# Cross-attention layer on one core: all 32 row tiles by seven half-size score products per pair, and the V side as whole float32 products

## The reference, cut to what matters

```python
Q = (img_embed @ Wq)...; K = (sent_embed @ Wk)...; V = (sent_embed @ Wv)...   # per head
score = einsum('bhqd,bhkd->bhqk', Q, K) / sqrt(D)
attn  = softmax(where(mask, score, -inf))
ctx   = einsum('bhqk,bhkd->bqhd', attn, V).reshape(B, -1, H * D)
out   = ctx @ Wo + img_embed
return (out - mean) * rsqrt(var + EPS) * gamma + beta
```

## Time and profile before

| | |
|---|---|
| median of three runs | 364.62 us |
| profiled execution, own time | 364.46 us |
| its span, first to last instruction | 362.6 us |
| TensorE busy | 353.9 us (98%) |
| VectorE / ScalarE / GpSimd busy | 296.4 (82%) / 238.3 (66%) / 193.1 (53%) |
| mean granted TensorE clock | 0.996 |

### The profile page before, as it was taken

One profiled execution on the slowest core, in us unless ns is written; L12 is line 12 of the kernel. 1 busy time (PEld: TensorE's weight loads), 2 busy tenths in 40 slices (PEclk: granted clock), 3 DMA queues, 4 the chain that ended last, 5 costly groups with the idle time before them and its releaser, 6 DMA issues.

```text
span 362.6 us, 6839 instructions
## 1 busy us (share of the span) xinstructions
PE 353.9 (98%) x2326; PEld 329.0 (91%) x2326; DVE 296.4 (82%) x516; ACT 238.3 (66%) x767; POOL 193.1 (53%) x180
## 2 busy tenths in 40 slices
PE   8999999999999999999999999899999999999993
PEld 5999999999999998999899988889988998998873
DVE  3489999998878587887888787797977978889886
ACT  3377757776876565765677667677768768767550
POOL 0046644654455212445355667597696696784234
PEclk9999999999999999999999999999999999999998
DMA  8998679966733310314234052231431423412012
GB/s 259 413 422 312 227 265 372 337 229 259 249 116 122 114 57 3 131 46 156 78 116 144 32 174 85 92 101 75 174 106 70 163 64 123 146 61 87 29 60 87
DMA packets 19682, 55.81 MB, mean 154 GB/s; under 512 B 1728, under 2 KB 3264, under 8 KB 17728
## 3 DMA queue, kind: packets, MB, share of 16 engines
q1 hardware_dynamic: 18784, 54.38, 42.2%
q10 hardware_dynamic: 864, 1.00, 0.9%
HBM read 46.98 MB, written 8.39 MB: 153 GB/s over the span
## 4 chain that ended last, share of the span: by engine, by line
PE 88%; DMA 4%; ACT 3%; DVE 2%; POOL 1%; issue 1%; POOLq 0%; DVEq 0%; ACTq 0%
PE pair L381 28%; PE pair L556 27%; PE pair L484 14%; PE pair L496 13%; PE pair L543 5%; DMA w_out<-wq_t 3%; PE pair L469 1%; DMA w_proj<-wk 1%; ACT prob L693 1%; ACT prob L715 1%; POOL out_sb L1158 1%; ACT centred L762 1%; PE pair L388 1%; PE pair L514 0%; DVE centred L1041 0%
## 5 line engine op out<-in xcount | busy, mean ns | idle before, releaser
L1205 POOL TENSOR_TENSOR w_proj_lo<-w_proj,w_proj_hi 128x768 fp32r<-128x768 f32 x26 | 47.9, 1866 | 61.1 <-ACT w_proj_hi L645 61.1
L693 ACT ACTIVATE prob<-masked,neg_max 128x77 f32<-128x77 f32 x128 | 44.2, 347 | 38.6 <-DVE neg_max L916 38.6
L381 PE MATMUL pair<-kv_t,w_out_hi 128*128 128x308 f32 x240 | 63.0, 335 | 0.3 <-DVE w_out_lo L849 0.3
L1158 POOL TENSOR_TENSOR out_sb<-centred,beta_sb 128x512 f32<-128x512 f32 x31 | 40.0, 1292 | 42.4 <-ACT centred L762 42.4
L556 PE MATMUL pair<-vw_hi,pt_hi 128*128 128x512 f32 x155 | 61.7, 398 | 0.0
L556 PE MATMUL pair<-vw_hi,pt_lo 128*128 128x512 f32 x155 | 60.8, 392 | 0.0
L556 PE MATMUL pair<-vw_lo,pt_hi 128*128 128x512 f32 x155 | 60.8, 392 | 0.0
L849 DVE TENSOR_TENSOR w_out_lo<-w_out,w_out_hi 128x1024 fp32r<-128x1024 f32 x30 | 49.3, 1682 | 4.9 <-ACT w_out_hi L653 4.4
L381 PE MATMUL pair<-kv_t,w_out_lo 128*128 128x154 f32 x240 | 48.8, 244 | 0.0
L381 PEld LDWEIGHTS pair<-kv_t,w_out_hi 128*128 128x128 f32 x240 | 42.2, 189 | 0.7 <-issue 0.7
L381 PEld LDWEIGHTS pair<-kv_t,w_out_lo 128*128 128x128 f32 x240 | 42.5, 189 | 0.0
(11 more groups left out here) (116 smaller groups left out, 954.8 us busy)
## 6 DMA issues: line engine op xcount, KB each, us to landing
w_out<-wo SPq DMA_DIRECT2D x8, 1024.0 KB, 5.1
xt_in<-x_tiles SPq DMA_DIRECT2D x16, 512.0 KB, 4.0
x_in<-x_rows SPq DMA_DIRECT2D x16, 512.0 KB, 4.6
out<-out_sb SPq DMA_DIRECT2D x31, 256.0 KB, 2.1
w_out<-wq_t SPq DMA_DIRECT2D x7, 1024.0 KB, 7.2
w_proj<-wv SPq DMA_DIRECT2D x8, 768.0 KB, 5.8
w_proj<-wk SPq DMA_DIRECT2D x6, 768.0 KB, 9.4
w_out<-wq_t SPq DMA_DIRECT2D x2, 512.0 KB, 7.8
```

The source lines that it names most:

```text
L381: mm = pe.matmul(pair[:, bank, 0:n], w[:, m, k, :], moving[:, k, 0:n], start=(at == 0), stop=(at == len(steps) - 1))
L693: e = act.activation(prob[i % 2][:, cols], masked[i % 2][:, cols], ACT.Exp, bias=neg_max[i % 2][:, h:h + 1], accum_out=sums[i % 2][:, h:h ...
L1158: pool.tensor_tensor(out_sb[i % OUT_RING][:, :], centred[i % 2][:, :], beta_sb[:, :], ALU.add)\
L1205: pool.tensor_tensor(half_cols(w_proj_lo[u % W_RING], half), half_cols(w_proj_sb[u % W_RING], half), half_cols(w_proj_hi[u % 2], half).bit ...
```

## The change

1. Pairs take all 32 tiles (16 pairs). `scores`, `mask_and_max`, `exps`, `split_xt` and the splitting of x by tile are gone; `mask_rows` has both batches.
2. Steps 8 to 15 use whole float32: `project_full` and `out_product_full`. The rounding and splitting of Wv, Wo, V and the adding of two halves of VW fall away.
3. The right sums of both batches are made by VectorE from a_hi and a_lo step by step (20 adds, 8 splits of 616 columns), during steps 8 to 11, in memory that is free then. T3 takes the place of the quarter of A that no product reads.
4. The x loads come later: the xt buffers hold right sums until those are split; x_in lies where the weight buffers were.

```diff
-    PAIRED = s.per_batch
-    NPAIRS = (T - PAIRED) // 2
+    NPAIRS = T // 2
+    T_STEPS = {T1: 3, T2: 5, T4: 7, T3: 10}
...
+        def whole(u):
+            return u < FULL_PROJ or u >= H
+        def whole_out(u):
+            return u < FULL_OUT or u >= H
...
+        def right_steps(b):
+            x, y, z = t_tmp[b]
...
+            return [(y, hi[0][1], hi[0][0], ALU.subtract), (z, y, lo[0][1], ALU.add), (x, z, lo[0][0], ALU.subtract),
+                    (z, hi[1][1], x, ALU.subtract), (y, z, lo[1][1], ALU.add),
+                    (z, hi[1][0], y, ALU.subtract), (x, z, lo[1][0], ALU.add),
+                    (z, hi[1][1], hi[0][1], ALU.subtract), (y, z, lo[1][1], ALU.add), (z, y, lo[0][1], ALU.subtract)]
...
             def load_xt(c):
+                if c < XT_RING:
+                    sp.wait_ge(act_t_hi, len(T_PARTS))
+                    sp.wait_ge(dve_t_lo, len(T_PARTS))
...
-            sp.wait_ge(pe_proj, 2 * USES)
+            for c in range(XT_RING):
+                load_xt(c)
+            sp.wait_ge(pe_outp, 2 * USES)
             for c in range(X_RING):
                 load_x(c)
...
             def first_products(p):
                 if p == 0:
-                    pe.wait_ge(dve_rows, 2)
-                    pe.wait_ge(act_t_hi, 4)
-                    pe.wait_ge(pool_t_lo, 4)
-                    pe.wait_ge(dve_masked, PAIRED)
+                    pe.wait_ge(dve_rows, 3)
+                    pe.wait_ge(act_t_hi, len(T_PARTS))
+                    pe.wait_ge(dve_t_lo, len(T_PARTS))
+                    wait_kv(USES - 1, 1)
+                    pe.wait_ge(dve_vw_lo, sum(len(part) for part in plan[:H - 1]))
...
+                if p == 0:
+                    transpose_vw(H)
+                    pe.wait_ge(dve_vw_lo, sum(len(part) for part in plan[:H]))
...
             for u in range(USES):
-                if u + 1 < FULL_PROJ:
+                if u + 1 < USES and whole(u + 1):
                     project_full(u + 1)
...
-                if u == USES - 1:
-                    pe.wait_ge(dve_a_lo, 2 * H)
-                    wait_kv(USES - 1, 1)
-                    scores(0)
-                if u < FULL_OUT:
+                if whole_out(u):
                     out_product_full(u)
...
-            scores(1)
-            pe.wait_ge(dve_vw_t, 2 * H)
-            transpose_vw(H)
-            transpose_prob(0)
-            for i in range(2, PAIRED - 1):
-                scores(i)
...
-                out_rows(i - 2)
-                transpose_prob(i - 1)
-            scores(PAIRED - 1)
+            first_products(0)
+            second_products(0)
+            first_products(1)
+            transpose_prob(0)
+            second_products(1)
+            pe.wait_ge(dve_vw_lo, len(groups))
+            out_rows(0)
+            transpose_prob(1)
+            for p in range(2, NPAIRS):
+                a = 2 * p
                 first_products(p)
                 transpose_prob(a - 2)
                 out_rows(a - 3)
...
+            copy_s1(0)
+            round_sums(1)
             split_vw(H)
+            exps_first(0)
+            copy_s1(1)
+            exps_second(0)
             split_pt(0)
+            round_blocks(2)
+            round_sums(2)
+            exps_first(1)
+            split_pt(1)
+            exps_second(1)
+            for p in range(2, NPAIRS):
...
             def combine_c22(p):
                 if p > 0:
-                    dve.wait_ge(act_exp, PAIRED + 2 * p)
+                    dve.wait_ge(act_exp, 2 * p)
```

More of the change, by code:

```diff
@@ L123, in lt @@
                 return late.enter_context(nc.sbuf_tensor(name, shape, dt))
-            t_hi = lt("t_hi", [P, 4, KT, s.half], F32R)
-            t_lo = lt("t_lo", [P, 4, KT, s.half], F32R)
-            two_ones = lt("two_ones", [P, P], F32R)
[L128 to L139, removed]
+            xo_lo0 = lt("xo_lo0", [P, 7, KT, P], F32R)
+            x_sum = lt("x_sum", [P, 4, KT, P])
+            xo_hi0 = lt("xo_hi0", [P, 7, KT, P], F32R)
+            xo_lo1 = lt("xo_lo1", [P, 7, KT, P], F32R)
+            lt("gap0", [P, 256])
+            xo_hi1 = lt("xo_hi1", [P, 7, KT, P], F32R)
+            lt("gap1", [P, 256])
+            mask_rows = lt("mask_rows", [P, s.batches, s.half], F32R)
+            two_ones = lt("two_ones", [P, P], F32R)
+            x_in = [lt(f"x_in{n}", [P, CHUNK, s.model]) for n in range(X_RING)]
+            xo_hi, xo_lo = [xo_hi0, xo_hi1], [xo_lo0, xo_lo1]
         with ExitStack() as raw:
@@ L160, in build @@
                          for n in range(2)]
[L161 to L164, removed]
+        t_hi0 = sb("t_hi0", [P, 3, KT, s.half], F32R)
+        t_lo0 = sb("t_lo0", [P, 3, KT, s.half], F32R)
+        t_hi1 = sb("t_hi1", [P, 3, KT, s.half], F32R)
+        t_hi, t_lo = [t_hi0, t_hi1], [t_lo0, t_lo1]
+        c12 = sb("c12", [P, s.half])
+        sb("gap2", [P, 288])
         prob1 = sb("prob1", [P, s.row])
@@ L178, in build @@
             w_out_hi = [w_out_hi0, w_out_hi1]
-        masked = [sb(f"masked{n}", [P, s.row]) for n in range(2)]
+        c2 = sb("c2", [P, s.row])
+        u2_w2 = sb("u2_w2", [P, 2, s.half])
+        u2, w2 = u2_w2[:, 0, :], u2_w2[:, 1, :]
         prob = [sb("prob0", [P, s.row]), prob1]
@@ L471, in transpose_vw @@
                     mm.then_inc(pe_vw, 1)
[L473 to L481, removed]
-                    for n, (xs, a) in enumerate(passes):
-                        for half in range(2):
-                            mm = pe.matmul(ps_scores[i % 2][:, half, 0:s.half], xs[:, k, :],
-                                           a[:, k, b, half * s.half:(half + 1) * s.half],
-                                           start=(k == 0 and n == 0),
-                                           stop=(k == s.model_t - 1 and n == len(passes) - 1))
-                mm.then_inc(pe_scores, 1)
             def product(p, bank, left, right_hi, right_lo, begin=True):
@@ L513, in first_products @@
                 pe.wait_ge(pool_xo_lo, SPLITS * p + 1)
-                pe.matmul(bank_a[:, 0:s.half], two_ones[:, :], mask_rows[:, :], start=True, stop=True)
-                product(p, bank_a, A11, right(a_hi, 0, 0), right(a_lo, 0, 0), False)
+                pe.matmul(bank_a[:, 0:s.half], two_ones[:, :], mask_rows[:, b, :], start=True, stop=True)
+                product(p, bank_a, A11, right(a_hi, b, 0, 0), right(a_lo, b, 0, 0), False)
                 pe.wait_ge(act_xo_hi, SPLITS * p + 3)
@@ L771, in _ @@
                     round_kv(u + 1)
-                if FULL_PROJ <= u + 2 < USES:
+                if u + 2 < USES and not whole(u + 2):
                     round_w_proj(u + 2)
-                if u == USES - 1:
-                    exps(0)
+                if u == H + 1:
+                    for part in T_PARTS[:4]:
+                        round_t(*part)
+                elif u in (H + 2, H + 3):
+                    for part in T_PARTS[2 * (u - H):2 * (u - H) + 2]:
+                        round_t(*part)
+                if u == USES - 2:
+                    round_blocks(0)
+                    round_sums(0)
+                elif u == USES - 1:
+                    round_blocks(1)
                 take_out_product(u, 0)
@@ L936, in right_sum @@
[L936 to L945 removed]
+                dve.wait_ge(dve_mask, 1)
```

425 lines of the change are left out of this document (199 added, 226 removed).

## The result

The changed kernel takes 363.36 us, median of 20 runs (362.93 to 364.92); the kernel before takes 364.62 beside it (364.24 to 365.37). The ratio is 0.9971 (95%: 0.9961 to 0.9981). By the medians it is 1.26 us faster, by the means (363.67 and 364.73), with which the ratio goes, 1.06, where 2.1 were forecast. The 363.36 lies in the range. The profiled execution took 363.32 us for a span of 361.5.

A forecast was written before the change was run, and what follows sets the result against it. TensorE, busy 98% of the span, was taken as the bound. Terms -5.5 + 2.3 - 0.3 - 1.2 + 2.8 gave -1.9 us, a second way -2.2; taken -2.1: 362.5 us, span 360.5, range 361.0 to 364.7.

The forecast's parts named there:

- part 4, (a): First pair waits for the mask rows behind the rests of VW of step 15: TensorE stalls 1.6 us.
- Part 1: Batch 0 scores by pairs, 43 matmuls instead of 48 for two tiles: -5.5 us for eight pairs more.
- Part 2: V steps as whole float32, 7.35 us instead of 7.06: +2.3 us for eight, -0.3 for a wait in step 14.
- Rival 4: Passes, not weight loads, set both products: whole float32 costs +15.7 us in place of +2.3, 375.9 us; chance 0.03.
- Part 3: Right sums on VectorE in V steps 8 to 11, adds at 0.8 us: cost 0 on the path, slack 2.5 us.
- Rival 3: Right sums at the contended price, 1.53 us an add: out products wait, 9 us in all, 371.5 us; chance 0.05.
- new waits: Waits at the beginning of the rows, in place of the old 1.20 us gap: 2.8 us, bounds 0.4 and 5.6.
- (c): Prob 0 is normalised 10.0 us after F, the first pair's start; TensorE is done at 9.8: stall 0.3 us.
- (d): TensorE waits for the split of prob 1, behind tile 0's residual and layer norm on VectorE: stall 0.7 us.
- (b): In pair 0 the banks are handed on by w2 and c22, each a VectorE step behind a product: 0.2 us.
- Rivals 1 and 2: 1: start hides nothing, waits 5.6, 365.3 us, chance 0.12. 2: start covered better, waits 1.2, 360.9 us, chance 0.10.
- the walk: Second way to the span: pair 0 begins at 126.2, pair 3 at 159.0, then pairs of 14.1: 360.4, or -2.2 us.

The follow-up runs named there:

- early rows: Changed kernel with the mask rows made on VectorE ahead of the rests of VW of step 15 instead of behind them: 360.85 us, again 360.76.
- GpSimd kept out: Changed kernel with GpSimd's first split of pair 1 waiting until the mask rows are made: 362.23 us, ratio 0.9936 to the kernel before.
- both edits: Changed kernel with mask rows made early and the split of prob 1 ahead of tile 0's residual and layer norm: 360.28 us, again 360.50.

## Why the prediction was off, step by step

The direction and most of the mechanisms held. The step that failed is part 4, (a), the wait for the mask rows: it was priced at 1.6 us and cost 2.31 by starts, since GpSimd stretched two_ones, and that a wait can also bring the lower clock was put at nothing and took 0.4 us from the mean.

- **Part 1, right.** Pairs 3, 4 and 5 begin at 160.12, 174.21 and 188.31, 14.09 and 14.10 us apart, and there is no wait at the old place.
- **Part 2, right, and one detail missed.** A V step takes 7.35 us in three profiles; alone the part costs +1.7, for the +2.3 and -0.3 of the working. Rival 4 is refuted: it had +15.7 us. The Trainium skill, "FP8 and Floating Point Precision", section "TensorE Precision Notes", has true float32 in four passes, from which the prediction estimated +14.4; the runs don't bear that out for the exchange, since the short product costs more than its columns. Not foreseen: out product 7, still short, takes 65.83 - 61.68 = 4.15 us behind a whole projection, not 65.30 - 61.28 = 4.02, of which the shorter projection ahead of it (3.05 for 3.15) gives 0.1 back.
- **Part 3, right.** All adds took 0.80 us, with GpSimd idle, and no out product waited. ScalarE waited for sums 2.6 us, at no cost. Rival 3 is refuted.
- **Part 4 (a), wrong in size.** From the transposes to the first pair I had 3.5 us, with two_ones at 0.20 as in the earlier trace rows. It took 4.13, since GpSimd's next split runs beside it: 1.06 from its start to that of the mask rows. I had used a stretched VectorE operation (1.53 against 0.80) for rival 3 alone, and did not ask which GpSimd work the end of the last block sets free. TensorE by itself needs 1.82 us there (1.9 in the working), as the run with early rows shows. So the wait, counted by starts as in the working, became 4.13 - 1.82 = 2.31. With GpSimd kept out it is 125.69 - 122.42 - 1.82 = 1.45: but for GpSimd the term was right to 0.15. Besides, the lower bound of the new waits is added up wrongly: 2.8 less 1.6 and half of (c) and (d) is 0.7, not 0.4; no range hangs on it.
- **Part 4 (a), its second price missed.** Behind the 2 us wait stands the 1.2 GHz level in one of three profiles of the changed kernel, and 16 of 39 executions have the mean clock and the time that go with it, 1.3 to 1.6 us more by the means of each group. The gap of 1.20 us in the kernel before brought it in none of 36 executions, and I took from it that a wait costs its length.
- **Part 4 (b) to (d), right.** Prob 0 is turned 10.05 us after F (forecast 10.1), the wait for pt_lo is 0.57 (0.7), three pairs take 32.95 (32.8). Rivals 1 and 2 are out.

The span was to be 360.5 and is 361.5. By pair 3, which begins 1.1 us later than in the walk, it adds up: 0.4 from the start of the execution, 0.7 of the wait and 0.15 in pairs 0 to 2, less 0.15 in the V steps, which by starts take 66.2 us with their transposes and not 66.4. The first is chance. project(3) begins at 22.90 in the profile before and at 23.30 in the one after, though the instructions ahead of it are the same; in the ten profiles of changed kernels it is at 22.7 to 23.5. What differs is visible: the first 48 records of whole float32 take 11.93 - 4.52 = 7.41 us in the profile after and 11.02 - 4.58 = 6.44 in the one before, and 0.5 of that is made up at out product 1, where the one before waits for its rests of w_out. Why those records differ stays open.

Over all executions it adds up without that chance: of the 2.1 us forecast the wait takes 0.7, and the lower clock, in 6 of 20 executions at 1.37 us, takes 0.4 of the mean. That leaves 1.0; the means differ by 1.06.

What beats both kernels is the version with both edits: 360.28 and 360.50 us, 1.2% under the kernel before and 3 us under the changed one.

Open: what decides whether the clock falls after 2.0 us. 2 of 7 executions on one chip and 8 of 12 on another may differ by the chip or by chance. The runs vary the length of the wait; what else at this change of phase helps to bring the lower clock was not separated.

## What to carry to other kernels

Price a wait that you add at a change of phase with what becomes free at the same moment: the instruction on the chain can be stretched by the engine that the same event releases. Look for the last small preparation on the chain that depends on nothing late, and move it ahead; here one call moved by a step was worth 2.5 us, twice the whole change. And where TensorE waits 2 us or more, compare the times of all executions and the granted clock behind the wait, not one profile: the median can hide a second price that only some runs pay.

## What the runs showed of the hardware

- By their mean clock and time, 16 of 39 executions fell to the 1.2 GHz level behind a TensorE wait of 2.0 us, 6 of 6 behind 3.4 us, and none of 61 with 1.2 us or less; two profiles show the fall itself. The Trainium skill, "TensorE: Matmul & The Clock Gate", section "HAM oscillation — how this bites in real kernels", says that idle gaps of TensorE, as between its tiles of K, take the clock down. The runs agree that a gap does it, and show the fall behind one of 2.01 us, shorter than those the page names.
- An add of 128 columns on VectorE (two_ones, from SBUF to SBUF) took 0.28 us with GpSimd at rest, and 1.14 and 0.79 beside an operation of 512 columns on GpSimd. Both times it ended 0.15 us after GpSimd's did (126.65 and 126.50; 120.41 and 120.26), though it began at different points of it, and GpSimd's took 1.29 and 1.28 us, for 1.30 without. That reads as VectorE held until GpSimd is done, not as both slowed; no run varied GpSimd's length to show it.
- A k-step of whole float32 with 154 columns takes 0.2625 us, one of short products with 308 and 154 columns 0.252: the short product saves 4%. The weight loads are busy all the time beside both (the earlier trace rows and the row after); that they set the price was not tested.
- With the same instructions ahead of it project(3) began at 22.68 to 23.48 us in ten profiles, a scatter of 0.8 us.
